# Asking for one batch's rows earlier, and putting one batch's shared up-projection ahead of the routed experts

## The chip, the cores and the metric

The kernel runs on one core of one Trainium2 chip. The metric is the device time of one execution in microseconds. Before the change three executions took 786.92, 786.30 and 786.67 us; the median is 786.67 us. A difference of about 0.2% (1.6 us) is what measurements of this kernel can tell from no change.

## The reference

The input is x, 8 batches of 512 tokens of 256 numbers. One transformer block is computed, in float32:

```python
x = x + _L0_attn_ref(_layernorm(x), W_Q, W_K, W_V, W_O)     # 16 heads of 16, causal softmax
x = x + _L0_ffn_ref(_layernorm(x), gate_w, w_gate_up, w_down, shared_w_gate, shared_w_up, shared_w_down, shared_gate_w)

# _L0_ffn_ref, with x as 4096 rows of 256
shared = jax.nn.silu(x @ shared_w_gate.T) * (x @ shared_w_up.T) @ shared_w_down.T     # 704 wide
shared = shared * jax.nn.sigmoid(x @ shared_gate_w.T)
probs = jax.nn.softmax(x @ gate_w.T, axis=-1)             # 16 experts
rw, sel = jax.lax.top_k(probs, 2)                         # two of them for each token
rw = rw / rw.sum(axis=-1, keepdims=True)
gu = jnp.einsum('nd,edf->nef', x, w_gate_up)              # each expert is 128 wide
g, h = jnp.split(gu, 2, axis=-1)
expert_out = jnp.einsum('nef,efd,ne->nd', jax.nn.silu(g) * h, w_down, combine)
out = expert_out + shared
```

`combine` holds rw at the two chosen experts of a token and zero elsewhere.

## The kernel before, in words

Every float32 product is made of three matmuls (`exact_product`, lines 186 to 188): each operand is split into a high part, rounded by ScalarE's copy, and a low part, the rest, subtracted by VectorE; high times high, high times low and low times high are added in PSUM.

There are two blocks, with a barrier of all engines between them: `build_attention` and `build_ffn`. Five engines run their own queues: TensorE (PE), VectorE (DVE), ScalarE (ACT), GpSimd (POOL) and SyncE (SP), which issues the plain DMAs in order. An engine waits at an instruction for a semaphore and everything behind it on that engine waits too.

The attention block goes through turns it = 0 to 8. Turn `it` holds steps of several batches; a table, `TURN`, sets their order. In the last turn (it = 8) only the remainder of batch 7's attention is left, together with the shared up-projection of batch 0 (steps U), and the last two chunks of shared weights are loaded and split: the load at line 344, ScalarE's copy at line 590 and GpSimd's subtraction at line 502. SyncE's part of a turn is `body(it)`. After the last turn SyncE waits until the attention's results x1 and xn2 (the normalised rows) are in DRAM, then loads xn2 of batch 1 into `xn_f` (line 409) and waits for it; only then is its part of the block over. `xn_f` was read before that by the transposes `fT` of batch 0.

The second block has these stages.

1. Routing (DVE lines 1269 to 1339): ranks, tiles and slots of the chosen tokens. When the slots are known, GpSimd scatters every token's row into `xg_dram`, 64 indirect DMAs of 128 rows each (line 1165), ordered by batch. The rows come through the buffer `srow`, which SyncE fills (line 1070).
2. Beside this, the first half of the shared expert, batches 0 to 3 (`FIRST` = 4). A batch b consists of `up(b)` (66 matmuls of 512 columns in 6 steps, for batch 0 done already in attention), the transposes of batch b + 1's rows (line 1491), and `down(b)` (72 matmuls of 256 columns). DVE makes h from ScalarE's silu (line 1383) and its low part (line 1386), and adds the result to x1 (`add_shared`, line 1366). Besides, the 16 experts' weights are split, one behind each step (ACT line 1212, DVE line 1418); `EXPERTS_FROM` says which in which batch.
3. The routed experts (`tiles`): 40 pairs of tiles of 128 rows. A pair is loaded from `xg_dram` (line 1085), transposed (line 1554), multiplied by gate and up weights, transposed again (line 1573), multiplied by the down weights, and stored into `yg_dram` (line 1089). They begin when all 64 scatters have landed. They end with the transposes of batch 4's rows.
4. The second half of the shared expert, batches 4 to 7. Beside it GpSimd gathers each token's two expert rows, 64 indirect DMAs (line 1177), two for each tile m of 128 tokens, m = 0 to 31 in order; DVE adds them to the sums (`add_first`, `add_second`, line 1402). The table `TILES_BESIDE` says how many tiles of 0 to 27 are added behind each step j of batches 4 to 7; tiles 28 to 31 are added at the very end, into `x1` of batch 7, then `add_shared(7)` is made and the last two stores go out (line 1134).

h's two parts lie in `heads_held` (`h_hi`, `h_lo`) and h itself in `rows_held`; the routed experts put their own two parts of h, `hT_hi` and `hT_lo`, into the same `h_hi` and `h_lo`.

Of the kernel before, what the change touches and what calls it, by code (L numbers as in the profile page):

```python
# [190 lines left out]
def build_attention(nc, ctx, ident, stacks, projected, w_lo, x_lower, rows_held, heads_held, x, wq, wk, wv, wo, gates, shared_up, shared_down, logits_all, top, index,  # L191
# [112 lines left out]
    def _(sp):  # L304
# [41 lines left out]
        def body(it):  # L346
            before, this, after = it >= 1, it < B, it + 1 < B
            if it + 2 < B:
                sp.wait_ge(xn_done, it + 2)
                sp.dma_start(xb[:, :, :], x_v[it + 2]).then_inc(x_in, 16)  # L350
            zero_rows(3 * it)
            zero_rows(3 * it + 1)
            if before:
                if it >= 2:
                    sp.wait_ge(x1_out, 16 * (it - 1))
                    sp.wait_ge(xn2_done, it - 1)
                sp.dma_start(x1[:, :, :], x_v[it - 1]).then_inc(xres_in, 16)
            if it == B - 1:
                shared_weights(0)
                shared_weights(1)  # L360
                sp.wait_ge(xn2_out, 16)
                sp.dma_start(xn_f, xn2_v[0]).then_inc(first_in, 16)
            if this:
                max_rows(it, 0)
            if after:
                stack_out_of_sbuf(it + 1, 0)
            zero_rows(3 * it + 2)
            if it == B:
                shared_weights(4)
                shared_weights(5)  # L370
            if after:
                stack_back(it + 1, 0)
            if it == B - 1:
                shared_weights(2)
                shared_weights(3)
            if after:
                stack_out_of_sbuf(it + 1, 1)
            if this:
                max_rows(it, 1)
            if before:  # L380
                sp.wait_ge(xn2_done, it)
# [24 lines left out]
        sp.wait_ge(zero_rows_out, 16 * ZERO_DMAS)  # L406
        sp.wait_ge(first_in, 16)
        sp.wait_ge(work_ready, plan.upto("ready", "fT", DK - 1))
        sp.dma_start(xn_f, xn2_v[1]).then_inc(first_in, 16)
        sp.wait_ge(first_in, 32)  # L410
# [496 lines left out]
PARITY = B // 2  # L907
EXPERTS_FROM = [0, 0, 6, 11, 16]
LOADS = 4
PER_LOAD = E // LOADS  # L910
TILES_BESIDE = {4: (0, 1, 1, 1, 1, 1, 2), 5: (1, 1, 1, 1, 1, 1, 1), 6: (1, 1, 1, 1, 1, 1, 1), 7: (1, 1, 1, 1, 1, 1, 1)}
assert sum(sum(v) for v in TILES_BESIDE.values()) == NT - TB

# [34 lines left out]
def build_ffn(nc, ctx, stacks, projected, w_lo, x_lower, rows_held, heads_held, logits_all, top, index, slots, experts_of_four, weight, gate, x1_dram, xn2_dram, xg_dram, yg_dram, y1_dram,  # L948
# [24 lines left out]
    args, exps, slot_f = (places[n].rearrange("p (c t) -> p c t", c=2) for n in ("args", "exps", "slot_f"))  # L973
    earlier, ones = sb("earlier", [P, P], bf16), sb("ones", [P, P], bf16)
    both, tiles_i = sb("both", [P, NT, E], bf16), sb("tiles_i", [P, E], mybir.dt.int32)
# [68 lines left out]
    def is_pair(q):  # L1044
        return 0 <= q < TILE_PAIRS
# [8 lines left out]
    def _(sp):  # L1054
# [6 lines left out]

        def load_next_xn(b, more):
            if b and more:
                sp.wait_ge(xT_ready, DK * b)
                load_xn(b + 1)
# [6 lines left out]
        def first_half(b, more):  # L1072
            load_next_xn(b, more)
            if b == 0:
# [37 lines left out]
        def second_half(b, more):  # L1112
# [4 lines left out]
            else:  # L1117
                load_y1(b - 1)
            load_next_xn(b, more)
            for j in range(FT + 1):  # L1120
# [60 lines left out]
    def _(act):  # L1181
# [4 lines left out]

        def shared(b, more, beside=None):

            if b == 0:
                return  # L1190
            for j in range(FT + 1):
                n = (b - 1) * FT + j
# [4 lines left out]
                if j > 0:  # L1197
# [3 lines left out]
                    act.activation(h_hi[0:filled(j - 1), j - 1, :], h[0:filled(j - 1), (j - 1) % 2, :], ACT.Copy).then_inc(h_hi_done, 1)  # L1201
                if beside and j >= 1:
                    beside(j - 1)
            if more:
                split_xT(b + 1)

        def first_half(b, more):
            def split_expert(i):
                e = EXPERTS_FROM[b] + i
# [26 lines left out]
        def slot(n):  # L1236
            if is_pair(n - 1):
                split_h(n - 1)
            if n >= 0:
                split_x(n + 2) if is_pair(n + 2) else split_xT(FIRST, [n + 2 - TILE_PAIRS]) if n + 2 < TILE_PAIRS + DK else None  # L1240
            if is_pair(n + 1):
# [18 lines left out]
    def _(dve):  # L1260
# [108 lines left out]
        def shared(b, more, beside):  # L1369

            if b == 0:
                for j in range(FT + 1):
                    routing(j)
                weights()
                return
            for j in range(FT + 1):
                n = (b - 1) * FT + j
# [10 lines left out]
                if j >= 1:  # L1388
                    beside(j - 1)
# [4 lines left out]
            if more:  # L1394
                split_xT(b + 1)
            beside(FT)
            add_shared(b)

# [14 lines left out]
        def first_half(b, more):  # L1413
            def split_expert(i):
                e = EXPERTS_FROM[b] + i
# [24 lines left out]
        def slot(n):  # L1440
            if is_pair(n - 1):
                lower_h(n - 1)
            if n >= 0:
                lower_x(n + 2) if is_pair(n + 2) else split_xT(FIRST, [n + 2 - TILE_PAIRS]) if n + 2 < TILE_PAIRS + DK else None
            if is_pair(n + 1):
                product(n + 1)

        def tiles():
            for q in range(2):
                lower_x(q)  # L1450
            slots_of_loop(slot)

        def second_half(b, more):
            def add_old(j):
                for m in tiles_beside(b, j):
# [26 lines left out]
    def _(pe):  # L1482
        def transpose_xn(b, ks=range(DK)):
# [3 lines left out]
            for k in ks:  # L1487
                if b == FIRST:
                    pe.wait_ge(m_xT_split, TILE_PAIRS - DK + k + 1)
# [12 lines left out]
        def shared(b, more):  # L1502
            if b:
                up(b)
            if b and more:
                transpose_xn(b + 1)
            down(b)

        def up(b):
# [76 lines left out]
        def slot(n):  # L1586
            if is_pair(n - 1):
                transpose_h(n - 1)
            if n >= 0:
                transpose_x(n + 2) if is_pair(n + 2) else transpose_xn(FIRST, [n + 2 - TILE_PAIRS]) if n + 2 < TILE_PAIRS + DK else None  # L1590
            if is_pair(n + 1):
# [4 lines left out]
        def tiles():  # L1596
            pe.wait_ge(xT_split, (FIRST - 1) * DK)
# [74 lines left out]
```

## Time and profile before

| what | value |
|---|---|
| median of three executions | 786.67 us |
| profiled execution: its own time | 787.38 us |
| profiled execution: span, first to last instruction | 785.6 us |
| PE busy | 706.8 us (90%) |
| DVE busy | 528.1 us (67%) |
| ACT busy | 400.7 us (51%) |
| POOL busy | 327.3 us (42%) |
| mean granted TensorE clock | 0.965 |

The span is what the rows of the trace are counted in; 1.8 us of the profiled execution lie around it. A PE row's duration is longer than the distance between two starts, because matmuls are pipelined: distances are read from start times. The granted clock is 1.00 where TensorE runs at 2.4 GHz throughout, 0.5 where it runs at 1.2 GHz. A group "A <- B" in a view of waits is time in which A stood idle until B released it.

### The profile page before, as it was taken

To read this page: it belongs to the slowest core of one execution; us is meant where nothing else is said; L and a number is where in the kernel's file an instruction comes from. 1 tells how busy PE (TensorE), PEld (TensorE's weight loads), DVE (VectorE), ACT (ScalarE), POOL (GpSimd) and SP (SyncE) were. 2 spreads that over 40 slices of the span, in tenths; PEclk is the share of its full clock that TensorE was granted. 3 is DMA by queue.
4 is the path that set the end of the run, shared out by engine and by line. 5 is a ranking of instruction groups with operands and counts; after the bars stand their busy time and mean duration, and the time that the engine had idled before them with its cause. 6 is when DMAs were issued, how large, how long until landed. Compare 5 with 4: busy or idle time off the path is not lost. (4 is left out here: it accounts for less than half of the span.)

```text
span 785.6 us, 16690 instructions
## 1 busy us (share of the span) xinstructions
PE 706.8 (90%) x5970; PEld 561.8 (72%) x5970; DVE 528.1 (67%) x1158; ACT 400.7 (51%) x779; POOL 327.3 (42%) x678
## 2 busy tenths in 40 slices
PE   1579999999999999999998687999499999899997
PEld 1446576676766767676665576888499999788886
DVE  6286788887888888787843677556155555367567
ACT  3116756666675657657665324334166666433222
POOL 5203527274452725625382227777200000177770
PEclk9888999999999999999999979999699999999999
DMA  5578657577774758747331297654555565378763
GB/s 155 197 265 280 232 191 251 184 257 251 265 254 163 270 182 296 243 176 250 98 101 60 80 344 271 203 199 153 183 168 189 190 185 175 134 217 270 248 187 120
DMA packets 102319, 159.84 MB, mean 203 GB/s; under 512 B 7520, under 2 KB 78176, under 8 KB 98016
## 3 DMA queue, kind: packets, MB, share of 16 engines
q1 hardware_dynamic: 96096, 141.99, 53.7%
q0 software_dynamic: 6144, 16.79, 6.6%
q8 instruction: 51, 0.84, 0.4%
q14 instruction: 28, 0.23, 0.1%
HBM read 86.66 MB, written 71.83 MB: 202 GB/s over the span
## 5 line engine op out<-in xcount | busy, mean ns | idle before, releaser
L657 DVE TENSOR_REDUCE neg_max<-ps_w 128x1 f32<-128x512 f32 (+3 forms) x352 | 202.7, 633 | 46.1 <-PE ps_w L762 46.0
L578 ACT ACTIVATE probs<-ps_w 128x512 f32<-128x512 f32 x320 | 165.4, 621 | 10.1 <-PE ps_w L778 10.0
L415 POOL TENSOR_TENSOR pool_scratch<-minus_half 1x1 f32<-1x1 f32 x190 | 34.8, 183 | 244.1 <-ACT probs L578 201.8
L1177 POOL DMA_INDIRECT ex<-yg_dram,slots x64 | 64.2, 1003 | 147.1 <-DMA yg_dram<-y 127.9
L447 POOL TENSOR_SCALAR_AFFINE_SELECT probs<-probs 128x256 f32<-128x256 f32 (+1 forms) x224 | 93.8, 430 | 0.0
L1165 POOL DMA_INDIRECT xg_dram<-srow,slots x64 | 67.5, 1055 | 33.8 <-issue 18.9
L1196 ACT ACTIVATE rows_held<-ps_f 128x512 f32<-128x512 f32 (+1 forms) x42 | 25.0, 596 | 107.8 <-PE ps_f L188 107.8
L789 PE MATMUL ps_w<-probs,v_aug 128*32 128x512 f32 (+3 forms) x1024 | 78.9, 450 | 0.9 <-DVE x_lower L621 0.6
L186 PE MATMUL ps_f<-stacks 128*128 128x512 f32 x154 | 61.5, 399 | 4.9 <-DVE rows_held L1383 4.9
L789 PEld LDWEIGHTS ps_w<-probs,v_aug 128*32 128x32 f32 x1024 | 31.4, 112 | 43.1 <-issue 34.1
L188 PE MATMUL ps_f<-stacks 128*128 128x512 f32 x154 | 60.7, 394 | 0.0
L187 PE MATMUL ps_f<-x_lower,stacks 128*128 128x512 f32 x154 | 60.7, 394 | 0.0
L586 ACT ACTIVATE o_raw<-ps_w 128x512 f32<-128x512 f32 x32 | 19.1, 597 | 76.2 <-PE ps_w L789 76.2
L1383 DVE TENSOR_TENSOR rows_held<-ps_f,rows_held 128x512 f32<-128x512 f32 (+1 forms) x42 | 29.0, 691 | 42.5 <-ACT rows_held L1196 42.3
L186 PE MATMUL ps_f<-stacks,heads_held 128*128 128x256 f32 (+1 forms) x192 | 56.7, 295 | 0.0
L187 PE MATMUL ps_f<-w_lo,heads_held 128*128 128x256 f32 (+1 forms) x192 | 54.9, 286 | 0.0
L188 PE MATMUL ps_f<-stacks,heads_held 128*128 128x256 f32 (+1 forms) x192 | 54.8, 285 | 0.0
L762 PE MATMUL ps_w<-mask_rows,ident_rows 64*128 64x128 bf16 (+2 forms) x704 | 53.2, 229 | 0.0
L754 PE MATMUL ps_w<-stacks 64*128 64x256 f32 (+3 forms) x256 | 41.6, 378 | 11.1 <-DMA stacks<-qk_dram 10.7
L186 PE MATMUL ps_f<-ex,stacks 128*128 x160 | 48.9, 306 | 0.8 <-DVE x_lower L1425 0.8
L188 PE MATMUL ps_f<-ex,x_lower 128*128 x160 | 45.6, 285 | 0.0
L187 PE MATMUL ps_f<-ex,stacks 128*128 x160 | 45.6, 285 | 0.0
(191 smaller groups left out, 1788.3 us busy)
## 6 DMA issues: line engine op xcount, KB each, us to landing
qk_dram<-projected SPq DMA_DIRECT2D x96, 256.0 KB, 5.7
stacks<-qk_dram SPq DMA_DIRECT2D x16, 1024.0 KB, 7.2
heads_held<-qk_dram SPq DMA_DIRECT2D x12, 1024.0 KB, 6.3
xg_dram<-zeros SPq DMA_DIRECT2D x20, 512.0 KB, 10.4
srow<-xg_dram SPq DMA_DIRECT2D x40, 256.0 KB, 2.9
ex<-experts SPq DMA_DIRECT2D x4, 1536.0 KB, 14.7
yg_dram<-projected SPq DMA_DIRECT2D x20, 256.0 KB, 2.1
yg_dram<-y SPq DMA_DIRECT2D x20, 256.0 KB, 2.2
```

The costliest lines, as they stand in the source:

```text
L186: pe.matmul(out, s_hi, m_hi, start=start, stop=False)
L187: pe.matmul(out, s_hi, m_lo, start=False, stop=False)
L188: return pe.matmul(out, s_lo, m_hi, start=False, stop=stop)
L415: ticks = Ticks(pool, pool_ticks, lambda: pool.tensor_tensor(out=pool_scratch[:, 0:1], in0=minus_half[0:1, 0:1], in1=minus_half[0:1, 0:1], ...
L447: masked = pool.affine_select(out=diagonal, in_=diagonal, compare_op=ALU.is_ge, fill=0.0, base=0, pattern=[[0, number], [1, P]], channel_m ...
L578: act.activation(probs[:, g, p * PAIR + half * BANK:p * PAIR + (half + 1) * BANK], ps_w[:, plan.bank(kind, which, half), :], ACT.Exp).then ...
L657: dve.tensor_reduce(out=neg_max[u][:, qt, first:first + len(heads)], in_=bank[:, 0:len(heads) * width].rearrange("p (h n) -> p h n", h=len ...
L754: pe.matmul(outs[half][:, i * width:(i + 1) * width], q_st[u][b % 2][rows, slot, qt * P:(qt + 1) * P], k_st[u][b % 2][rows, slot, 0:width] ...
L762: made = pe.matmul(blocks, ident_rows[rows, part, :], mask_rows[rows, part, first:P].unsqueeze(1).to_broadcast([ROWS, len(heads), P - first]),
L789: made = pe.matmul(out[hh * STRIP:(hh + 1) * STRIP, kt * P:S], v_aug[b % 2][:, kt, group * GH + hh, :], probs[:, g, pair * PAIR + col:pair ...
L1165: pool.indirect_dma_start(out=xg_rows, out_offset=bass.IndirectOffsetOnAxis(ap=slots[:, c, n:n + 1], axis=0), in_=srow[:, b % 2, t, :], in ...
L1177: pool.indirect_dma_start(out=back[:, m, c, :], out_offset=None, in_=yg_rows, in_offset=bass.IndirectOffsetOnAxis(ap=slots[:, c, m:m + 1], ...
```

## The change

1. In the attention block SyncE asks for `xn_f` of batch 1 inside turn 8, right behind the last two weight loads, instead of behind the last stores.
2. `up(4)` of the shared expert, with the silus, the products and the splits that belong to it, stands ahead of the routed experts, behind `down(3)`; its `down(4)` stays behind them. The transposes of batch 4's rows move ahead of `down(3)`, and those of batch 5's rows take their place at the end of the routed experts.
3. The experts' weights are split 4, 4, 4 and 4 in batches 1 to 4 instead of 6, 5 and 5 in batches 1 to 3. The tiles of the gather go 1, 9, 9 and 9 beside batches 4 to 7 instead of 7, 7, 7 and 7.
4. Because batch 4's h is kept through the routed experts, `hT_hi` and `hT_lo` get other places; the routing's `both`, `earlier` and `ones` are moved into `rows_held` to make room.

```diff
             if it == B:
                 shared_weights(4)
                 shared_weights(5)
+                sp.wait_ge(first_in, 16)
+                sp.wait_ge(work_ready, plan.upto("ready", "fT", DK - 1))
+                sp.dma_start(xn_f, xn2_v[1]).then_inc(first_in, 16)
...
         sp.wait_ge(zero_rows_out, 16 * ZERO_DMAS)
-        sp.wait_ge(first_in, 16)
-        sp.wait_ge(work_ready, plan.upto("ready", "fT", DK - 1))
-        sp.dma_start(xn_f, xn2_v[1]).then_inc(first_in, 16)
         sp.wait_ge(first_in, 32)
...
-EXPERTS_FROM = [0, 0, 6, 11, 16]
+EXPERTS_FROM = [0, 0, 4, 8, 12, 16]
...
-TILES_BESIDE = {4: (0, 1, 1, 1, 1, 1, 2), 5: (1, 1, 1, 1, 1, 1, 1), 6: (1, 1, 1, 1, 1, 1, 1), 7: (1, 1, 1, 1, 1, 1, 1)}
+TILES_BESIDE = {4: (0, 0, 0, 0, 0, 0, 1), 5: (1, 1, 1, 2, 1, 1, 2), 6: (1, 1, 2, 1, 1, 2, 1), 7: (1, 1, 2, 1, 2, 1, 1)}
...
-    hT_hi, hT_lo = (v[:, 0:2, 0:2 * P] for v in (h_hi, h_lo))
+    hT_hi, hT_lo = w_lo[:, 3], sb("hT_lo", [P, 2, 2 * P], f32r)
...
-            sp.wait_ge(xT_ready, DK * (FIRST - 1))
-            load_xn(FIRST)
+            sp.wait_ge(xT_ready, DK * FIRST)
+            load_xn(FIRST + 1)
...
+            if b in (0, FIRST):
                 return
+            activations(b, beside)
+            if b < B - 1:
+                split_xT(b + 1)
+            if b == FIRST - 1:
+                activations(FIRST, beside)
...
+            if b == FIRST:
+                add_shared(b)
+                for j in range(FT + 1):
+                    beside(b, j)
+                return
+            products(b, beside)
+            if b < B - 1:
+                split_xT(b + 1)
+            beside(b, FT)
+            add_shared(b)
+            if b == FIRST - 1:
+                products(FIRST, beside)
...
         def tiles():
+            dve.wait_ge(h_split, FIRST * FT)
             for q in range(2):
                 lower_x(q)
...
         def shared(b, more):
-            if b:
+            if b not in (0, FIRST):
                 up(b)
-            if b and more:
-                transpose_xn(b + 1)
+                if b < B - 1:
+                    transpose_xn(b + 1)
             down(b)
+            if b == FIRST - 1:
+                up(FIRST)
...
-            pe.wait_ge(h_done, (FIRST - 1) * FT)
+            pe.wait_ge(h_done, FIRST * FT)
```

`activations` and `products` are the loops over the steps that stood in ScalarE's and DVE's `shared` before.

How SyncE's queue reads at the end of the attention block, first before, then in the changed kernel (line numbers shift by a few):

```order
L357 DMA x<-x 128x4x256
L344 DMA projected<-shared_down 128x768 x2
L382 DMA xn_dram<-xn 128x4x256
L387 DMA x_dram<-x 128x4x256
L409 DMA projected<-xn_dram 128x4x256
L1632 UNCONDITIONAL_BRANCH
```

In the changed kernel, the same place of SyncE's queue:

```order
L357 DMA x<-x 128x4x256
L344 DMA projected<-shared_down 128x768 x2
L373 DMA projected<-xn_dram 128x4x256
L385 DMA xn_dram<-xn 128x4x256
L390 DMA x_dram<-x 128x4x256
L1654 UNCONDITIONAL_BRANCH
```

The load into `projected` (where `xn_f` lies) went from behind the two last stores to ahead of them.

DVE's queue before, from the last step of batch 3 to the first pair of the routed experts (L1386 is the low part of h, L1418 an expert's split, L1366 `add_shared(3)`, L1425 the low part of a pair's rows):

```order
L1383 TENSOR_TENSOR rows_held<-ps_f,rows_held 64x512
L1386 TENSOR_TENSOR heads_held<-rows_held,heads_held 128x512
L1418 TENSOR_TENSOR ex<-ex 128x768
L1386 TENSOR_TENSOR heads_held<-rows_held,heads_held 64x512
L1366 SCALAR_TENSOR_TENSOR projected<-ps_f,gate,projected 128x256 x4
L1425 TENSOR_TENSOR x_lower<-ps_f,stacks 128x512 x2
L1432 TENSOR_TENSOR rows_held<-ps_f,rows_held 128x256
```

The same engine in the changed kernel, from the low parts of batch 4's rows (L1351) and `add_shared(3)` (L1374) on:

```order
L1351 TENSOR_TENSOR x_lower<-ps_f,stacks 128x512 x2
L1374 SCALAR_TENSOR_TENSOR projected<-ps_f,gate,projected 128x256 x4
L1406 TENSOR_TENSOR rows_held<-ps_f,rows_held 128x512 x2
L1409 TENSOR_TENSOR heads_held<-rows_held,heads_held 128x512
L1437 TENSOR_TENSOR ex<-ex 128x768
...
L1437 TENSOR_TENSOR ex<-ex 128x768
L1406 TENSOR_TENSOR rows_held<-ps_f,rows_held 64x512
L1409 TENSOR_TENSOR heads_held<-rows_held,heads_held 128x512
L1409 TENSOR_TENSOR heads_held<-rows_held,heads_held 64x512
L1444 TENSOR_TENSOR x_lower<-ps_f,stacks 128x512 x2
L1451 TENSOR_TENSOR rows_held<-ps_f,rows_held 128x256
```

Batch 4's six products and six low parts, with the last four expert splits among them, now stand between `add_shared(3)` and the first pair. No expert split stands between batch 4's last two low parts.

TensorE's queue before, at the end of `down(3)` (256 columns), where the first transposes of the routed experts follow:

```order
L186 MATMUL ps_f<-stacks,heads_held 128x256
L187 MATMUL ps_f<-w_lo,heads_held 128x256
L188 MATMUL ps_f<-stacks,heads_held 128x256
L1554 MATMUL ps_f<-ident,srow 128x128 x8
```

In the changed kernel, the end of `down(3)` with the first of `up(4)`'s 66 matmuls of 512 columns behind it:

```order
L186 MATMUL ps_f<-stacks,heads_held 128x256
L187 MATMUL ps_f<-w_lo,heads_held 128x256
L188 MATMUL ps_f<-stacks,heads_held 128x256
L186 MATMUL ps_f<-stacks 128x512
L187 MATMUL ps_f<-x_lower,stacks 128x512
L188 MATMUL ps_f<-stacks 128x512
```

`up(4)` took the place of the transposes, which follow behind it.

## Rows read from the trace of the kernel before

**Rows 1.** Windows: busy us (instructions) of PE, PEld, DVE, ACT, POOL, clock, DMA, GB/s.

```profile
500.00:520.00 20.00, 20.00 (x112) 17.42 (x111) 13.85 (x21) 11.33 (x19) 15.73 (x15) 1.00 0.65 228
540.00:560.00 20.00, 8.55 (x70) 8.24 (x69) 5.52 (x10) 2.47 (x5) 12.15 (x12) 0.81 0.46 160
```

**Rows 2.** Chain that ended last: start us, us, what; scatters, then the first pair.

```profile
490.18 1.41 POOL xg_dram L1165
...
554.54 2.40 DMA xg_dram<-srow,slots
...
559.83 1.10 PE ps_f L1554 x4
```

**Rows 3.** Timeline, the first pairs of the routed experts.

```profile
559.83 1.94 PE L1554 MATMUL ps_f<-ident,srow 128*128 128x128 f32 x8 [11.45 <-DMA srow<-xg_dram]
562.54 0.57 PE L186 MATMUL ps_f<-ex,stacks 128*128 x1 [0.78 <-DVE x_lower L1425]
565.26 0.98 PE L1554 MATMUL ps_f<-ident,srow 128*128 128x128 f32 x4
567.73 0.60 PE L1554 MATMUL ps_f<-ident,srow 128*128 128x128 f32 x4
570.54 0.60 PE L1554 MATMUL ps_f<-ident,srow 128*128 128x128 f32 x4
```

**Rows 4.** Timeline, PE, end of down(3): start us, us, engine, line, operation.

```profile
547.87 0.28 PE L186 MATMUL ps_f<-stacks,heads_held 64*128 64x256 f32 x1
```

**Rows 5.** The gathers' line: durations ns, first and last start, landing.

```profile
L1177 POOL DMA_INDIRECT ex<-yg_dram,slots x64: 942/946/1360, 683.4 to 765.9; - x64
DMA to landing us min/median/max: 2.6/4.0/7.4
```

**Rows 6.** Timeline, the end of the program.

```profile
778.04 3.25 DVE L1402 SCALAR_TENSOR_TENSOR projected<-ex,weight,projected 128x256 f32<-128x256 f32 x8
780.24 0.28 PE L186 MATMUL ps_f<-stacks,heads_held 64*128 64x256 f32 x1
781.33 1.66 DVE L1366 SCALAR_TENSOR_TENSOR projected<-ps_f,gate,projected 128x256 f32<-128x256 f32 x4
```

**Rows 7.** Timeline, end of the attention block and start of the second.

```profile
448.30 0.36 SPq L409 DMA_DIRECT2D projected<-xn_dram  x1
448.40 1.80 POOL L502 TENSOR_TENSOR w_lo<-projected,stacks 128x768 fp32r<-128x768 f32 x1 [6.49 <-ACT stacks L590]
452.65 0.15 POOL L1150 IOTA projected<- 128x16 f32 x1 [2.44 <-POOLq L1632]
```

**Rows 8.** Waits of SyncE's queue, 405 to 453: us in total, times, longest.

```profile
SPq L382 <- DVE xn L606: 31.5, 1, 31.5
SPq L1632 <- DMA projected<-xn_dram: 3.5, 1, 3.5
```

**Rows 9.** Timeline, PE: starts of up(6), of two of its triples, and of up(7).

```profile
731.78 0.50 PE L186 MATMUL ps_f<-stacks 128*128 128x512 f32 x1
733.97 0.39 PE L186 MATMUL ps_f<-stacks 128*128 128x512 f32 x1
734.65 0.39 PE L186 MATMUL ps_f<-stacks 128*128 128x512 f32 x1
756.67 0.50 PE L186 MATMUL ps_f<-stacks 128*128 128x512 f32 x1
```

**Rows 10.** Page, groups of instructions: busy us, mean ns, idle before; a step's silu and product.

```profile
L1196 ACT ACTIVATE rows_held<-ps_f 128x512 f32<-128x512 f32 (+1 forms) x42 | 25.0, 596 | 107.8 <-PE ps_f L188 107.8
...
L1383 DVE TENSOR_TENSOR rows_held<-ps_f,rows_held 128x512 f32<-128x512 f32 (+1 forms) x42 | 29.0, 691 | 42.5 <-ACT rows_held L1196 42.3
```

**Rows 11.** Timeline, PE, last pair of the routed experts and first triples of up(4).

```profile
678.36 0.38 PE L186 MATMUL ps_f<-ex,heads_held 128*128 x1 [1.29 <-DVE heads_held L1437]
...
679.56 0.63 PE L186 MATMUL ps_f<-stacks 128*128 128x512 f32 x1
...
682.11 0.39 PE L186 MATMUL ps_f<-stacks 128*128 128x512 f32 x1
```

More of the change, by code:

```diff
@@ L973, in build_ffn @@
     args, exps, slot_f = (places[n].rearrange("p (c t) -> p c t", c=2) for n in ("args", "exps", "slot_f"))
-    earlier, ones = sb("earlier", [P, P], bf16), sb("ones", [P, P], bf16)
-    both, tiles_i = sb("both", [P, NT, E], bf16), sb("tiles_i", [P, E], mybir.dt.int32)
+    routed_by = rows_held[:, 0].bitcast(bf16)
+    both = routed_by[:, 0:NT * E].rearrange("p (t e) -> p t e", t=NT)
+    earlier, ones = (routed_by[:, NT * E + n * P:NT * E + (n + 1) * P] for n in range(2))
+    tiles_i = sb("tiles_i", [P, E], mybir.dt.int32)
     xT_hi, silu, h, h_hi, h_lo = shared_views(stacks, rows_held, heads_held)
@@ L1060, in load_x1, with load_next_xn @@
             sp.dma_start(x1[:, :, :], item(x1_v, b)).then_inc(x1_in, 16)
-        def load_next_xn(b, more):
-            if b and more:
+        def load_next_xn(b):
+            if b not in (0, FIRST, B - 1):
                 sp.wait_ge(xT_ready, DK * b)
@@ L1072, in first_half @@
         def first_half(b, more):
-            load_next_xn(b, more)
+            load_next_xn(b)
             if b == 0:
@@ L1118, in second_half @@
                 load_y1(b - 1)
-            load_next_xn(b, more)
+            load_next_xn(b)
             for j in range(FT + 1):
@@ L1185, in split_xT, with shared, activations @@
                 act.activation(xT_hi[:, k, :], ps[:, k, :], ACT.Copy).then_inc(xT_hi_done, 1)
-        def shared(b, more, beside=None):
-            if b == 0:
+        def shared(b, more, beside=lambda b, j: None):
+            if b in (0, FIRST):
                 return
+            activations(b, beside)
[3 more added lines that the diff above has]
+                activations(FIRST, beside)
+        def activations(b, beside):
             for j in range(FT + 1):
@@ L1201, in shared, with split_expert @@
                     act.activation(h_hi[0:filled(j - 1), j - 1, :], h[0:filled(j - 1), (j - 1) % 2, :], ACT.Copy).then_inc(h_hi_done, 1)
[L1202 to L1205, printed above, removed]
+                if j >= 1:
+                    beside(b, j - 1)
         def first_half(b, more):
-            def split_expert(i):
+            def split_expert(b, i):
                 e = EXPERTS_FROM[b] + i
@@ L1239, in slot @@
             if n >= 0:
-                split_x(n + 2) if is_pair(n + 2) else split_xT(FIRST, [n + 2 - TILE_PAIRS]) if n + 2 < TILE_PAIRS + DK else None
+                split_x(n + 2) if is_pair(n + 2) else split_xT(FIRST + 1, [n + 2 - TILE_PAIRS]) if n + 2 < TILE_PAIRS + DK else None
             if is_pair(n + 1):
@@ L1375, in shared, with products @@
                 return
+            if b == FIRST:
[10 more added lines that the diff above has]
+                products(FIRST, beside)
+        def products(b, beside):
             for j in range(FT + 1):
@@ L1388, in shared @@
                 if j >= 1:
-                    beside(j - 1)
+                    beside(b, j - 1)
                 if b == 1 and j == 1:
@@ L1393, in shared @@
                     experts_of_tiles()
[L1394 to L1397, printed above, removed]
         def add_rows(c, m, done):
@@ L1413, in first_half, with split_expert @@
         def first_half(b, more):
-            def split_expert(i):
+            def split_expert(b, i):
                 e = EXPERTS_FROM[b] + i
@@ L1443, in slot @@
             if n >= 0:
-                lower_x(n + 2) if is_pair(n + 2) else split_xT(FIRST, [n + 2 - TILE_PAIRS]) if n + 2 < TILE_PAIRS + DK else None
+                lower_x(n + 2) if is_pair(n + 2) else split_xT(FIRST + 1, [n + 2 - TILE_PAIRS]) if n + 2 < TILE_PAIRS + DK else None
             if is_pair(n + 1):
@@ L1453, in second_half, with add_old @@
         def second_half(b, more):
-            def add_old(j):
+            def add_old(b, j):
                 for m in tiles_beside(b, j):
@@ L1487, in transpose_xn @@
             for k in ks:
-                if b == FIRST:
+                if b == FIRST + 1:
                     pe.wait_ge(m_xT_split, TILE_PAIRS - DK + k + 1)
@@ L1502, in shared @@
         def shared(b, more):
-            if b:
+            if b not in (0, FIRST):
                 up(b)
-            if b and more:
-                transpose_xn(b + 1)
+                if b < B - 1:
+                    transpose_xn(b + 1)
             down(b)
+            if b == FIRST - 1:
+                up(FIRST)
         def up(b):
@@ L1589, in slot @@
             if n >= 0:
-                transpose_x(n + 2) if is_pair(n + 2) else transpose_xn(FIRST, [n + 2 - TILE_PAIRS]) if n + 2 < TILE_PAIRS + DK else None
+                transpose_x(n + 2) if is_pair(n + 2) else transpose_xn(FIRST + 1, [n + 2 - TILE_PAIRS]) if n + 2 < TILE_PAIRS + DK else None
             if is_pair(n + 1):
@@ L1596, in tiles @@
         def tiles():
-            pe.wait_ge(xT_split, (FIRST - 1) * DK)
+            pe.wait_ge(xT_split, FIRST * DK)
             for q in range(2):
                 transpose_x(q)
-            pe.wait_ge(h_done, (FIRST - 1) * FT)
+            pe.wait_ge(h_done, FIRST * FT)
             pe.wait_ge(y_done, FIRST * TB)
```

## The prediction

> **What bounds the kernel now.** I read the windows by stage first, then the chain that ended last, then the timelines at the stages' borders. The windows show TensorE busy for all of 500 to 520 us at a granted clock of 1.00, but for only 8.55 of the 20 us from 540 to 560, at 0.81 [rows 1]. In the chain the reader is to see who owns that hole: GpSimd's scatters. The last 48 (batches 2 to 7) start between 490.18 and 554.54, one in 1.369 us, the last lands 2.40 us later, its rows are read back, and TensorE's first transposes come at 559.83 [rows 2] after 11.45 us of idleness [rows 3]. `down(3)` had ended there: its row at 547.87 is the third-last triple, with two matmuls of it still to come, so about 548.3 [rows 4]. So up to 559.8 GpSimd bounds, after it TensorE: through the routed experts at 2.8 us a pair (567.73 to 570.54) [rows 3] and through the last four shared batches. GpSimd's gathers run beside these from 683.4 to 765.9 [rows 5], and the program's end follows TensorE and DVE: last matmuls about 780.6, DVE's last eight adds from 778.04, `add_shared(7)` at 781.33, end at 785.6 [rows 6]. The gathers have some 12 us of slack there. That slack is what decides this change.
>
> **The earlier load.** Before, SyncE issues it at 448.30 [rows 7] and waits 3.5 us for it at the block's end [rows 8]; the second block starts on GpSimd at 452.65 [rows 7]. In the new place the load is in flight while SyncE anyway waits 31.5 us for xn2 [rows 8]; its own condition, the transposes `fT`, belongs to the start of the turn. So the load's wait goes entirely. What is late next is GpSimd's last split of shared weights, from 448.40 to 450.20 [rows 7]. SyncE had been released at about 448.66 + 3.5 = 452.16; the barrier now waits for 450.20, so the second block starts 2.0 us earlier, not the 3.9 us that the load took. Bounds: 0 (the end of GpSimd's queue slips) and 3.9. I take 2.0. Everything in the second block up to `down(3)` hangs on the block's start through routing and the order of loads, so it moves by the same 2.0: `down(3)` ends at 546.3, the last scatter lands near 555, the first pair's rows are in near 557.8. Batches 1 to 3 now hold 12 expert splits instead of 16, which leaves DVE and ScalarE freer; I count nothing for it, as TensorE does not wait between 500 and 520 anyway [rows 1].
>
> **up(4) ahead of the experts.** It is 66 matmuls of 512 columns, 22 triples. A triple takes 734.65 - 733.97 = 0.68 us at full clock [rows 9], so up(4) takes 22 x 0.68 = 15.0 us. Its rows of xn are asked for behind the store of batch 2 and land while TensorE is in `up(3)`; it starts at 546.3 and ends at T = 561.3. Of its 15.0 us, 557.8 - 546.3 = 11.5 lie in the hole and 3.5 stick out. Behind T the pair's rows can be transposed at once, but the first pair's matmuls need DVE's low part of them, and DVE now stands behind the last products of batch 4 (the DVE order in the section on the change): silu, product, copy, low part, then the pair's low part, five operations in a row on two engines, of 0.60 us on ScalarE and 0.69 on DVE [rows 10]: 2 x 0.60 + 3 x 0.69 = 3.3, with the semaphores between them 3.5. I take T + 3.5 = 564.8. Bounds: T + 2.7, as without the products the way from the first transpose to the first matmul took 562.54 - 559.83 = 2.71 [rows 3], and T + 5, if two more operations of DVE are in the way. Against 562.54 [rows 3] that is 2.3 us late.
>
> The clock gives some back. Before, the hole left it low: the first 12 matmuls took 565.26 - 562.54 = 2.72 us, where the next 12 and their transposes took 567.73 - 565.26 = 2.47 together [rows 3]. 12 matmuls at full clock are about half of 2.72, 1.4 us, and the transposes behind them lose another 0.3: the low clock cost some 1.65 us. In the changed kernel TensorE stands idle only for about 2.5 us between its transposes and the first pair. The nearest case is the start of up(4): behind a wait of 1.29 us, two triples (the rows are the first's and the third's) took 682.11 - 679.56 = 2.55 us instead of 1.36 [rows 11], 1.2 us lost. I charge 1.2 here. So the routed experts run 2.3 - 1.65 + 1.2 = 1.8 us later than before; bounds 0 and 4.5.
>
> **The new places of hT_hi, hT_lo and the routing's tiles** change no instruction's shape: 0, for the 40 pairs bounded at -0.1 and +0.1 us each, since TensorE fills its 2.8 us period.
>
> **The second half.** TensorE sheds up(4) (15.0 us), the low clock at its start may stay with `down(4)` instead, and one set of transposes moves. up(6) to up(7) is 756.67 - 731.78 = 24.9 us for a whole batch [rows 9]. By TensorE alone the last matmul would come at 780.6 - 15.0 - about 2 + 1.8 = 765.4, and the end at about 770.5. But the gathers start on the last pair's store and do not get shorter: the last one is issued at 765.9 + 1.8 = 767.7. It lands 2.6 to 7.4 us later, in the median 4.0 [rows 5]; with little other traffic at that point I take 3.5: 771.2. Then DVE adds that tile's first row, and the four second ones: 5 of the 8 adds that took 3.25 us [rows 6], 2.1 us with their waits, 773.3. From `add_shared(7)`'s start to the end of the span it was 785.6 - 781.33 = 4.3 us [rows 6]. End: 777.6.
>
> In that half the other tiles are no obstacle: tile m is gathered at 683.4 + 2.62 (m + 1) + 4, the table asks for 9 tiles a batch of 24.9 us, that is one in 2.77 us, and starts about 10 us later than before. TensorE could wait a microsecond or two for DVE or for xn and still be ahead of the gathers.
>
> **Sum.** Span 777.6 against 785.6, so -8.0 us; the profiled time 787.38 would be 779.4. It was 0.7 over the median; the median goes from 786.67 to 778.7.
>
> One rule could speak against it. The gathers were issued one in (765.9 - 683.4)/63 = 1.309 us, of 942 ns at least and 1360 at most [rows 5], and the scatters, beside a denser DVE, one in 1.369 [rows 2]; so something beside them costs them time, and DVE's adds now stand closer together. The Trainium skill, "SBUF — State Buffer", in its rules on the shared port pair, says that GpSimd cannot write the descriptors of its DMAs while DVE holds the shared ports in a two-port mode, and that an operation with two SBUF inputs, which these adds are, takes only the read side, which it infers to leave descriptors alone. No run here separates the two. If the adds held it up, a gather would lose time with each add that falls on it, which is the last rival.
>
> **The rivals.**
>
> - *The gathers don't bind, TensorE does.* For: 15 us of its work go. Against: last gather at 765.9 [rows 5] plus the 5.6 us that must follow before `add_shared(7)`. It would need the gathers 7 us faster, one in 1.20 us, and the shortest distance is 0.95 + 0.30 = 1.25. Span about 770.5, time 771.6.
> - *The experts start later than reckoned.* The tail behind up(4), an expert split that holds DVE, or a longer spell of low clock: 4.5 us late instead of 1.8. Then the end is 780.3, the time 781.4. If the block's start gains nothing as well: 783.4.
> - *up(4) fills nothing.* Its rows or its banks come late (the xn load stands behind a store in SyncE's queue), so that it starts only when the scatters end, or it runs at the lower clock and takes 30 us. Start of the pairs at 557.8 + 15.0 + 3.5 = 576.3, 11.5 us behind the forecast: the gathers carry that to the end, span 789.1, time 790.2; with a quarter of it in the hole, 787.3, no change. Against: xn(b + 1) came in time in every batch of the first half, as TensorE never waited from 500 to 520 [rows 1].
> - *Slower: GpSimd's rate.* The last gather sets the end, so every 0.1 us on the distance between gathers costs 6.3 us. It decides from 1.309 + 8.0/63 = 1.436 on. The longest gather with its gap, 1.36 + 0.30 = 1.66 [rows 5], shows that single ones reach it. If DVE's adds, now in three batches instead of four, made the mean 1.45, the last would be issued at 767.7 + 8.9: span 786.5, time 787.6. Against: in both stages the mean stayed at 1.37 or below, and the number of DVE instructions beside the 64 gathers falls, as batch 4's products are gone.
>
> **How the numbers follow.** The forecast 0.66; experts later 0.14; TensorE binds 0.06; up(4) fills nothing 0.03, or about a quarter of what it could, which is no change, 0.05; slower by GpSimd's rate 0.06. Faster by more than 0.2% (below 785.1, about what a measurement of this kernel can tell from no change) is 0.66 + 0.14 + 0.06 = 0.86; same 0.05; slower 0.09. The range goes from 774.5 (block another 1.9 us earlier, landing after 2.6, no clock lost) to 783.4 (experts late, nothing gained at the block's start).
>
> **What would show it.** Right: the second block's first instruction near 450.6; no hole of TensorE between 546 and 561; first pair's matmul near 564.8; last gather issued near 767.7; DVE waiting for gathers at the very end, `add_shared(7)` directly behind the adds, and TensorE's last matmul some 7 us before it. Wrong: a wait of TensorE inside up(4), pairs above 2.85 us, gathers at another distance than 1.3, or DVE's last wait on TensorE.

## The result, and the profile after

The changed kernel takes 781.92 us in the median of 7 executions (779.22 to 783.88), against 786.67 us of the kernel before in 7 (784.40 to 788.29). The ratio is 0.9941 with a 95% interval of 0.9921 to 0.9960: 4.7 us faster. Two later series gave 0.9937 [0.9919, 0.9956] and 0.9935 [0.9916, 0.9954]. Forecast were 778.7 us (ratio 0.990) and a range of 774.5 to 783.4: the time lies in the range, and the gain is 4.7 us where 8.0 were forecast. The time is nearer to that of the rival with late experts (781.4) than to the forecast.

The profiled execution took 783.88 us, the slowest of the seven, with a span of 782.1 us against 785.6. Two rows of its windows answer to [rows 1] (columns as there):

```profile
540.00:560.00 20.00, 20.00 (x122) 17.77 (x121) 10.57 (x17) 6.58 (x13) 11.53 (x12) 1.00 0.46 155
560.00:580.00 20.00, 16.32 (x112) 15.37 (x111) 12.22 (x20) 11.42 (x24) 0.00 (x0) 0.91 0.35 114
...
760.00:782.00 22.00, 11.22 (x83) 10.49 (x81) 14.64 (x32) 2.86 (x5) 10.84 (x11) 0.80 0.45 140
```

The hole of 540 to 560 us, where TensorE had been busy for 8.55 us, is full and at full clock. A smaller one stands behind it, and a new one at the very end, where TensorE has 11.22 of 22 us.

At the border of the blocks the timeline shows (start us, us, engine, line, operation, idle time before and its releaser):

```profile
444.57 0.38 SPq L385 DMA_DIRECT2D xn_dram<-xn  x1
449.92 1.80 POOL L502 TENSOR_TENSOR w_lo<-projected,stacks 128x768 fp32r<-128x768 f32 x1 [6.49 <-ACT stacks L590]
452.06 0.15 POOL L1152 IOTA projected<- 128x16 f32 x1 [0.34 <-POOLq L1654]
```

SyncE's wait for its load is gone, and GpSimd goes on 0.34 us after its own last split, where it stood idle for 2.44 us in [rows 7]. From the store of batch 7's xn2 to the second block's start it is 452.06 - 444.57 = 7.49 us; it was 452.65 - 443.06 = 9.59. The store of before, which [rows 7] leave out:

```profile
443.06 0.38 SPq L382 DMA_DIRECT2D xn_dram<-xn  x1
```

The 2.1 us are what was forecast (2.0). But the store itself came 1.5 us later than before. One row of each timeline shows where that began; after:

```profile
404.69 3.90 PE L789 MATMUL ps_w<-probs,v_aug 128*32 128x512 f32 x32 [1.80 <-POOL probs L447]
```

and before, the same 32 matmuls:

```profile
404.70 2.36 PE L789 MATMUL ps_w<-probs,v_aug 128*32 128x512 f32 x32 [0.26 <-DVE logits_all L685]
```

They started at the same time and took 3.90 instead of 2.36 us, in a stretch at a granted clock of 0.71 (405 to 410) where the one of before had 1.00. TensorE had stood idle for 1.80 us ahead of them, where it was 0.26 before. The moved load is issued only at 413.96 us. So this is no effect of the change: over all 13 profiled executions of this case the store came between 441.3 and 445.1 us, with and without the moved load.

Behind the border, the chain that ended last has the transposes of batch 4's rows in it, ahead of `down(3)` (start us, us, what):

```profile
539.02 0.87 PE ps_f L1511 x8
```

and the timeline behind up(4), whose last matmul starts at 563.52, is this:

```profile
563.60 0.83 ACT L1220 ACTIVATE ex<-ex 128x768 fp32r<-128x768 f32 x1
563.75 1.04 PE L1576 MATMUL ps_f<-ident,srow 128*128 128x128 f32 x8
...
564.34 0.57 ACT L1206 ACTIVATE rows_held<-ps_f 64x512 f32<-64x512 f32 x1
...
564.47 0.96 DVE L1437 TENSOR_TENSOR ex<-ex 128x768 fp32r<-128x768 f32 x1
...
565.46 0.69 DVE L1406 TENSOR_TENSOR rows_held<-ps_f,rows_held 64x512 f32<-64x512 f32 x1
566.07 1.46 DVE L1409 TENSOR_TENSOR heads_held<-rows_held,heads_held 128x512 fp32r<-128x512 f32 x2
...
567.56 1.29 DVE L1444 TENSOR_TENSOR x_lower<-ps_f,stacks 128x512 fp32r<-128x512 f32 x2
568.47 0.58 PE L186 MATMUL ps_f<-ex,stacks 128*128 x1 [3.68 <-DVE x_lower L1444]
```

ScalarE's last expert split (L1220) stands ahead of the last silu (L1206), DVE's (L1437) ahead of the last product (L1406). TensorE waits 3.68 us and starts the first pair at 568.47, 5.9 us later than in [rows 3]. The gathers' line, against [rows 5]:

```profile
L1179 POOL DMA_INDIRECT ex<-yg_dram,slots x64: 942/949/1421, 689.0 to 772.9; - x64
...
DMA to landing us min/median/max: 2.7/3.9/7.0
```

They start 5.6 us later and the last comes 7.0 us later: the distance grew from 1.309 to (772.93 - 688.99)/63 = 1.332 us. Last, DVE's queue at the end, against [rows 6]:

```profile
770.58 0.48 DVE L1421 SCALAR_TENSOR_TENSOR projected<-ex,weight,projected 128x256 f32<-128x256 f32 x1 [0.35 <-DMA ex<-yg_dram,slots]
774.35 0.48 DVE L1421 SCALAR_TENSOR_TENSOR projected<-ex,weight,projected 128x256 f32<-128x256 f32 x1 [3.29 <-DMA ex<-yg_dram,slots]
775.72 2.07 DVE L1421 SCALAR_TENSOR_TENSOR projected<-ex,weight,projected 128x256 f32<-128x256 f32 x5 [0.88 <-DMA ex<-yg_dram,slots]
777.82 1.66 DVE L1374 SCALAR_TENSOR_TENSOR projected<-ps_f,gate,projected 128x256 f32<-128x256 f32 x4
```

DVE waits for gathers, makes five adds behind the last one, and goes into `add_shared(7)`. TensorE's last matmul starts at 770.95, 6.9 us ahead of that; before it was 0.85 us (780.48 against 781.33). The two last matmuls, after and before:

```profile
770.95 0.28 PE L188 MATMUL ps_f<-stacks,heads_held 64*128 64x256 f32 x1
```

```profile
780.48 0.28 PE L188 MATMUL ps_f<-stacks,heads_held 64*128 64x256 f32 x1
```

The gathers have taken the end over from TensorE.

### The profile page after: what moved, and what is told of

Same layout as the page of the kernel before. It is cut to its first block and busy times, and to the rows that moved or that the text cites. A ratio compares the mean times of both kernels' runs of the same rounds, so it can differ in the third digit from the quotient of the medians.

```text
span 782.1 us, 16692 instructions
## 1 busy us (share of the span) xinstructions
PE 707.3 (90%) x5970; PEld 562.6 (72%) x5970; DVE 527.6 (67%) x1158; ACT 400.8 (51%) x779; POOL 329.1 (42%) x678
## 5 line engine op out<-in xcount | busy, mean ns | idle before, releaser
L1206 ACT ACTIVATE rows_held<-ps_f 128x512 f32<-128x512 f32 (+1 forms) x42 | 25.0, 596 | 115.0 <-PE ps_f L188 115.0
L1406 DVE TENSOR_TENSOR rows_held<-ps_f,rows_held 128x512 f32<-128x512 f32 (+1 forms) x42 | 29.0, 691 | 39.4 <-ACT rows_held L1206 39.1
```

## The experiments

Each ratio is to the kernel before, measured on the same chip.

**Each part alone.** e1 is the kernel before with the moved load only:

```diff
+                sp.wait_ge(first_in, 16)
+                sp.wait_ge(work_ready, plan.upto("ready", "fT", DK - 1))
+                sp.dma_start(xn_f, xn2_v[1]).then_inc(first_in, 16)
...
-        sp.dma_start(xn_f, xn2_v[1]).then_inc(first_in, 16)
```

> The kernel before with only the load of batch 1's rows moved into the last turn. My theory: the barrier waits for GpSimd's last split instead of SyncE's load, the second block starts 2.1 us earlier counted from the same point of the last turn (TensorE's transposes of batch 7's xn2), and everything behind moves with it: ratio 0.9973. Rival 'given back': the scatters or experts' loads set the later times by themselves and the gain is lost before the end, ratio 1.000.

Measured: 0.9976 [0.9964, 0.9988], 785.30 us. In its timeline:

```profile
441.30 0.38 SPq L385 DMA_DIRECT2D xn_dram<-xn  x1
...
446.64 1.80 POOL L502 TENSOR_TENSOR w_lo<-projected,stacks 128x768 fp32r<-128x768 f32 x1 [6.49 <-ACT stacks L590]
...
448.78 0.15 POOL L1150 IOTA projected<- 128x16 f32 x1 [0.34 <-POOLq L1632]
```

From store to start 7.48 us, as in the changed kernel. The medians differ by 1.7 us (787.00 against 785.30); the interval is 0.9 to 2.8 us, so it holds the 2.1, and the rival without a gain lies outside it.

e2 is the changed kernel with that load put back at the end of the block:

> The changed kernel with the load of batch 1's rows back at the end of the attention block: the hoist of up(4) alone. My theory: the two parts add up, this one is worth 0.9941/0.9973 = 0.997, some 2.5 us. Rival 'the load is needed by the hoist': no gain at all, 1.000.

Measured: 0.9951 [0.9933, 0.9970], 783.45 us, with 9.52 us from store to start. The parts add up: 0.9976 x 0.9951 = 0.9927, within the intervals of 0.9935 to 0.9941. The medians put the hoist of up(4) at 3.2 us (786.60 against 783.45), the ratio at 3.9, and the interval of 2.4 to 5.3 still holds the 2.5 expected. Counted from the second block's start, which leaves the attention block's clock out, the rest of the program takes 330.0 us in e2 as in the changed kernel (330.1), and 333.0 in the kernel before: 2.9 us for the hoist.

**The changed kernel again**, as the yardstick:

> The changed kernel once more, as the yardstick for its neighbours of this call. Both theories: ratio to before 0.991 to 0.996. Theory 'clock accident': of its span, the attention part before the moved load is the same work as before, so the second block's start differs from that of before by -2.1 us plus whatever the clock did in the attention block (it was +1.5 in the first profile); the sum of both varies by a microsecond or two from one execution to the next. Rival 'the moved load disturbs attention': the second block again starts only about 0.6 us earlier than before.

Measured: 0.9937 [0.9919, 0.9956], 782.54 us. Its store came at 443.64 and its second block started at 451.12, again 7.48 us behind.

**The tail behind up(4).** e3:

```diff
-EXPERTS_FROM = [0, 0, 4, 8, 12, 16]
+EXPERTS_FROM = [0, 0, 6, 11, 16, 16]
```

> The changed kernel with the 16 expert splits again in batches 1 to 3 (6, 5, 5) and none beside up(4). Theory 'a split holds the tail': from the first transpose of the first pair to its first matmul it was 4.7 us with ScalarE's and DVE's last expert splits ahead of the last silu and product; without them 3.5 us, the last gather 1.2 us earlier, and as the gathers set the end the span 1.2 us shorter: 0.9985 of the changed kernel. Rival 'the chain of batch 4's own last step is that long': still 4.5 us and no difference.

Measured: 0.9915 [0.9894, 0.9936], 780.63 us, beside 782.54 us of the changed kernel on the same chip. Its timeline:

```profile
561.92 0.59 ACT L1206 ACTIVATE rows_held<-ps_f 64x512 f32<-64x512 f32 x1 [0.24 <-PE ps_f L188]
...
562.62 0.69 DVE L1406 TENSOR_TENSOR rows_held<-ps_f,rows_held 64x512 f32<-64x512 f32 x1
563.23 1.46 DVE L1409 TENSOR_TENSOR heads_held<-rows_held,heads_held 128x512 fp32r<-128x512 f32 x2
...
564.72 1.29 DVE L1444 TENSOR_TENSOR x_lower<-ps_f,stacks 128x512 fp32r<-128x512 f32 x2
565.62 0.38 PE L186 MATMUL ps_f<-ex,stacks 128*128 x1 [2.86 <-DVE x_lower L1444]
```

Counted from the last start in up(4), the first pair comes after 565.62 - 561.50 = 4.12 us instead of 568.47 - 563.52 = 4.95. So the splits held the tail, by 0.8 us and not by the 1.2 expected; the rest is the chain of batch 4's own last step. The medians differ by 1.9 us, but the two intervals overlap widely, so it is the trace that gives the 0.8.

e4 takes e3 and puts the first pair's split ahead of the last products of batch 4. Its core:

```diff
                 pe.wait_ge(h_done, (b - 1) * FT + max(j - 1, 0))
+                if b == FIRST and j == FT - 1:
+                    for q in range(2):
+                        transpose_x(q)
...
# ScalarE, behind the silu of step j; DVE likewise with lower_x(0), behind the product
+                if b == FIRST and j == FT - 1:
+                    split_x(0)
...
-            pe.wait_ge(h_done, FIRST * FT)
+            pe.wait_ge(h_done, FIRST * FT - 1)
```

> As e3, and besides the first pair's high and low parts stand ahead of the last products and low parts of batch 4 on ScalarE and DVE (TensorE transposes the first two pairs ahead of up(4)'s last step). If the gathers set the end and they start when the experts end, each us gained at the first pair is a us of the span: first matmul of a pair about 2.2 us behind up(4)'s end instead of 4.9, less clock lost, span 2.7 to 4 us below the changed kernel (ratio to before about 0.990). If TensorE set the end, less than 1 us.

Measured: 0.9884 [0.9864, 0.9904], 778.73 us. Its timeline, where L1228 and L1447 are the first pair's high and low parts:

```profile
564.85 0.59 ACT L1206 ACTIVATE rows_held<-ps_f 64x512 f32<-64x512 f32 x1 [1.15 <-PE ps_f L188]
565.34 0.58 ACT L1228 ACTIVATE stacks<-ps_f 128x512 fp32r<-128x512 f32 x1
565.47 0.69 DVE L1407 TENSOR_TENSOR rows_held<-ps_f,rows_held 64x512 f32<-64x512 f32 x1 [0.97 <-ACT rows_held L1206]
...
566.19 0.69 DVE L1447 TENSOR_TENSOR x_lower<-ps_f,stacks 128x512 fp32r<-128x512 f32 x1
...
567.10 0.38 PE L186 MATMUL ps_f<-ex,stacks 128*128 x1 [2.29 <-DVE x_lower L1447]
```

The pair starts 567.10 - 564.41 = 2.69 us behind up(4)'s last start. As the transposes now lie inside up(4), the fair measure is from `down(3)`'s last matmul: 18.69 us in e4, 19.22 in e3, 20.05 in the changed kernel. The gain by the trace is 1.4 us, not the 2.7 to 4 expected. The medians promised 3.8 us (782.54 against 778.73), so it was measured again, beside the changed kernel:

> e4 once more, next to the changed kernel on one chip. Theory: counted from the last matmul of down(3), its first pair starts 18.7 us later instead of 20.05, and the gathers begin 1.4 us earlier: 0.9965 to 0.998 of the changed kernel, 0.990 to 0.992 of before. Rival 'the second measurement was luck': the same as the changed kernel, 0.994.

> The changed kernel as the neighbour of e9. Both theories: 0.994 of before.

Measured: e9 0.9906 [0.9886, 0.9925], 779.62 us; the changed kernel 0.9935 [0.9916, 0.9954], 781.98 us. e9's pair starts 18.68 us behind `down(3)`. This is the version that beats both kernels, by 2.4 us and 7.8 us: its slowest execution (780.62) is faster than the fastest of the changed kernel beside it (781.52). Of the 2.4 us the traces account for 1.4; the rest stays open.

**Do the gathers set the end?** e5 leaves out the second gather of each token in the changed kernel (the second row added is not the chosen expert's), e6 does the same in the kernel before. The waits that count the gathers are halved with them and not shown here:

```diff
-            for c in range(2):
+            for c in range(1):
                 pool.indirect_dma_start(out=back[:, m, c, :], ...)
```

> The changed kernel with only the first of each token's two expert rows gathered (32 indirect DMAs instead of 64; the second row that is added is not the right one). Theory 'the gathers set the end': TensorE's last matmul and DVE's adds follow TensorE now, the end comes about 5 us behind TensorE's last matmul as it did before: last matmul near 771 in the profile, span near 776, 5 to 7 us below the changed kernel, 0.986 to 0.988 of before. Rival 'TensorE or DVE set the end anyway': within 1 us of the changed kernel.

> The same cut in the kernel before (32 gathers; the second row is not the right one). There the gathers had 12 us of slack, and TensorE once waited 1.2 us for rows whose load stood behind a late gather: theory: 1 us or less faster, 0.998 to 1.000. Rival: the gathers cost TensorE time by contention in both kernels, then here too 4 us or more go, 0.995 or less.

Measured: e5 0.9883 [0.9861, 0.9905], 777.50 us; e6 1.0004 [0.9989, 1.0019], 786.76 us. The end of e5:

```profile
768.28 3.25 DVE L1421 SCALAR_TENSOR_TENSOR projected<-ex,weight,projected 128x256 f32<-128x256 f32 x8
...
769.49 0.28 PE L188 MATMUL ps_f<-stacks,heads_held 64*128 64x256 f32 x1
771.57 1.66 DVE L1374 SCALAR_TENSOR_TENSOR projected<-ps_f,gate,projected 128x256 f32<-128x256 f32 x4
```

DVE makes its last eight adds in one go without a wait for a gather, as before the change in [rows 6]; `add_shared(7)` starts 2.1 us behind TensorE's last matmul, where it was 0.85 before and 6.9 in the changed kernel. Leaving these gathers out is worth 4 to 5 us in the changed kernel, a little less than the 5 to 7 expected, and nothing in the one before (0.9989 to 1.0019): the gathers bind only after the change, and in the kernel before they cost TensorE no time that reaches the end.

**What slows the gathers.** e7 makes DVE's adds beside them thin:

```diff
+            part = slice(0, D if b == B - 1 else 2)
-            dve.scalar_tensor_tensor(out=total, in0=back[:, m, c, :], ...
+            dve.scalar_tensor_tensor(out=total[:, part], in0=back[:, m, c, part], ...
```

> The changed kernel with DVE's adds of tiles 0 to 27 made on 2 of 256 columns only (the rest of those outputs is left out); tiles 28 to 31 as they are. Theory 'DVE's adds slow GpSimd's gathers': the distance between gathers falls from 1.332 us to 1.26 and the last comes 4 us earlier, span 4 us shorter. Rival 'other instructions of DVE or the DMA traffic slow them': the distance stays at 1.30 or above, span within 1.5 us of the changed kernel.

Measured: 0.9915 [0.9893, 0.9937], 780.11 us. From first to last gather 771.44 - 689.38 = 82.06 us, a distance of 1.303. That lies by the rival's number, yet the stream is shorter than the 83.0 to 83.9 us that it took in the three profiles of the changed kernel. The run did not decide it. What DVE did beside each gather of the changed kernel tells more. One of the slowest is this:

```profile
737.75 0.68 DVE L1409 TENSOR_TENSOR heads_held<-rows_held,heads_held 128x512 fp32r<-128x512 f32 x1
737.84 1.41 POOL L1179 DMA_INDIRECT ex<-yg_dram,slots  x1 [0.30 <-issue]
738.35 0.48 DVE L1421 SCALAR_TENSOR_TENSOR projected<-ex,weight 128x256 f32<-128x256 f32 x1
738.86 0.48 DVE L1421 SCALAR_TENSOR_TENSOR projected<-ex,weight,projected 128x256 f32<-128x256 f32 x1
```

The low part of h (L1409) and the adds (L1421) read two tiles of SBUF each; the products (L1406) and `add_shared` (L1374) read one of SBUF and one of PSUM. All 18 gathers above 1.05 us lay beside L1409 or L1421; not every gather beside them was slow, but none beside the others alone: the 24 that had neither of the two beside them took 0.99 us at most. The same holds for the 14 slow ones of the kernel before (L1386 and L1402 there), and all 13 that were left in e7, with its adds thin, lay beside L1409. So e8 makes both kinds thin, the adds as in e7 and the low parts of h in batches 5 to 7:

```diff
+                    some = slice(0, 2 if b > FIRST else S)
-                    dve.tensor_tensor(out=h_lo[0:filled(j - 1), j - 1, :], ...
+                    dve.tensor_tensor(out=h_lo[0:filled(j - 1), j - 1, some], ...
```

> As e7, and DVE's low parts of h in batches 5 to 7 are made on 2 of 512 columns too (those outputs are left incomplete). In the changed kernel every gather that took over 1.05 us lay beside an addition of two SBUF tiles (the adds or the low parts of h), and none beside DVE's other work did. Theory 'operations with two SBUF inputs hold the gathers up': with both kinds thin the distance falls to 1.26, the last gather is issued 4.5 us earlier than in the changed kernel counted from the first one, and the span is about 5 us shorter than the changed kernel's, 0.988 of before. Rival 'DMA traffic slows them, the coincidence is that both sit in the same steps': the distance stays at 1.30 as in e7, 0.9915.

Measured: 0.9867 [0.9843, 0.9892], 776.93 us. Its gathers:

```profile
L1179 POOL DMA_INDIRECT ex<-yg_dram,slots x64: 942/946/986, 687.7 to 766.6; - x64
```

None is above 986 ns, the distance is (766.55 - 687.71)/63 = 1.251 us, and 83.9 - 78.8 = 5.1 us of the stream are gone; against e10, measured beside it, it is 83.0 - 78.8 = 4.1 us, and the medians of the two differ by 5.05. From 689 to 767 us the DMA engines were no less busy (0.82 of the time against 0.77 in the changed kernel), so their traffic has no measurable share.

## Why the prediction was right, and where its sizes were off

The mechanism was the forecast one: SyncE's wait goes and GpSimd's split is late next; up(4) fills the hole and sticks out; the experts start later; the gathers, which had slack, carry that to the end and keep the larger part of TensorE's 15 us. The mechanism holds; several terms of the sum were mis-sized, by some 3 us together. The steps, against the profile:

- *The block's start, -2.0.* Right: -2.10 from the store on, in each profile with the moved load, and it reaches the end (e1). The profiled execution hid 1.5 us of it by the clock in the attention block.
- *`down(3)` moves with the block.* Wrong by 0.9 us. The transposes of batch 4's rows now stand ahead of `down(3)`, and I moved them in the text without paying for them. From block start to `down(3)`'s last matmul it was 548.11 - 452.65 = 95.46 us and is 548.42 - 452.06 = 96.36. Seven of the nine other profiles with the moved transposes have 96.1 to 96.4; the other two have 97.6, and e1, without them, 96.7 instead of 95.5. These three lost 1.2 us to the clock: 32 to 40 us behind the block's start they were granted 0.57, where the rest had 0.79.
- *up(4), 15.0 us.* Right: 548.63 to 563.52 for the starts, without a wait.
- *First pair at T + 3.5.* With T = 548.63 + 15.0 it was T + 4.8, near the bound of T + 5. I had looked only at whether a split stood between the last two low parts; the ones ahead of the last silu and product cost 0.8 us (e3). The other 0.5 are the chain, which I had summed without the low part of the step before.
- *The clock gives 1.65 back and takes 1.2.* Wrong as a pair of terms, and harmless only because both were near each other. The wait of 3.68 us ahead of the first pair cost as much as the long hole did. The first pair's 12 matmuls took 571.19 - 568.47 = 2.72 us at a granted clock of 0.50, as long as in [rows 3]; up to the next transposes it was 573.53 - 568.47 = 5.06 us against 567.73 - 562.54 = 5.19:

```profile
571.19 0.85 PE L1576 MATMUL ps_f<-ident,srow 128*128 128x128 f32 x4
...
573.53 0.60 PE L1576 MATMUL ps_f<-ident,srow 128*128 128x128 f32 x4
```

  So 0.13 us came back and not 0.45. From the first pair's first matmul to the first gather it was 683.44 - 562.54 = 120.90 us and is 120.52, which looks like the forecast gain, but e1, without the hoist, has 120.39 too, and over the 13 profiles the distance scatters from 120.2 to 121.4.
- *The experts late by 1.8.* The gathers, which follow them, start 688.99 - 683.44 = 5.55 us late in the profile. The 3.7 between are 1.4 of the attention part's clock (the block started at 452.06, not at 450.65), 0.9 of the transposes, 1.3 of the tail and 0.1 on the way to the first gather.
- *Gathers at an unchanged distance.* 1.332 instead of 1.309, 1.5 us over the 63. This was the mechanism of the last rival at a sixth of its size, and e8 shows that it is at work. How much the change added to it is less sure: in the two other profiles of the changed kernel (after_again and e10) the distance was 1.318 and 1.317, 0.5 us over the 63.
- *Landing after 3.5, then 2.1 and 4.3.* From the last gather's issue to the next add 2.8, then 2.1 and 4.3: 0.7 us better.

Together 1.4 + 0.9 + 1.3 + 0.1 + 1.5 - 0.7 = 4.5 us, which is the difference of the spans, 782.1 - 777.6. Without the clock's 1.4, which the median does not have to share, 3.1 are left, and the median missed by 3.2. That they agree so closely is in part luck: by the other two profiles 1 us of the 1.5 is scatter.

The rival in which TensorE sets the end did not come: it is 6.9 us ahead. That up(4) fills nothing did not either. The one with experts later than reckoned named the right term, the tail; net of the attention part's clock they were 4.1 us late, nearer its 4.5 than the forecast 1.8, as the measured time is nearer its 781.4.

On the rule weighed in the prediction: the Trainium skill, "SBUF — State Buffer", section "Who interferes with whom", says on the shared port pair that an operation with two SBUF inputs contends with a GpSimd instruction that reads SBUF, and infers that it leaves descriptor writing alone. For indirect DMAs, whose offsets (`slots`) lie in SBUF, the trace agrees with the first: they took up to 1.42 us beside such operations and 0.99 at most without them (e8). So the inference does not keep the issue of an indirect DMA free of such operations. Whether the reading of the offsets or the writing of descriptors is held up, no run here separates.

## What to carry to other kernels

Work moved into an idle stretch is paid by its critical tail, not by its matmuls: look at every instruction that stands ahead of the last product on the engines that feed the next stage, and put the next stage's first small operations ahead of it (e3 and e4 took back 1.4 us by the trace). Before shortening a bound engine, look up the slack of the stream beside it: of the 15.4 us from the last gather to `add_shared(7)` before, 4.9 are needed for its landing and five adds, which leaves 10.5 us of slack (and not the 12 I spoke of), not the 15 us of work taken off TensorE. The gathers' later start took 5.55 of the slack and their longer stream 1.5; the 3.5 that are left are what the span gained. And account in full for instructions that change places between two stages, the transposes too.

## What the hardware showed that I had not expected

A gather of 128 rows issued by GpSimd takes 0.95 us, with a gap of 0.30 behind it, but up to 1.42 us beside VectorE operations that read two SBUF tiles; in the changed kernel 18 of 64 took over 1.05 us, and none over 0.99 once those operations were thin, which shortened the stream by 4.1 to 5.1 us. Beside operations with one operand in PSUM alone it took no longer (12 of the 64, 0.95 us each), though these are as long (0.69 us for L1406, 0.68 for L1409).

The point of time at which the same attention code ended varied by 3.8 us between 13 profiled executions of these kernels (the store of batch 7's xn2 between 441.3 and 445.1 us). In the two compared here 1.5 us of it came in one stretch of 32 matmuls, 3.90 us at a granted clock of 0.71 against 2.36 at 1.00. With differences of a few microseconds, the distance between two fixed points of the trace tells more than the span.
